# Loading the last full group in four chunks, counting landed chunks on ScalarE, and ten tail pieces instead of fourteen

## The reference

```python
keep = (u >= P_DROP).astype(x.dtype)          # P_DROP = 0.1
x_drop = x * keep / (1.0 - P_DROP)            # x, u: 8192 x 64, fp32
y = x + jnp.matmul(adj, x_drop)               # adj: 8192 x 8192, fp32
m = jnp.mean(y, axis=-1, keepdims=True)
v = jnp.var(y, axis=-1, keepdims=True)
out = (y - m) / jnp.sqrt(v + 1e-5)
```

## Time and profile before

| | |
|---|---|
| median of 3 runs | 644.17 us (644.09 to 645.23) |
| the profiled execution's own time | 644.2 us |
| its span, from the first to the last instruction | 642.4 us |
| TensorE busy | 508.3 us, 79% |
| HBM read, written | 272.63 MB, 2.10 MB |
| mean granted TensorE clock | 0.906 |

### The profile page before, as it was taken

The page is one execution under the profiler, slowest core; times in us unless marked ns, Lnnn a source line. Parts: engine busy times, 40 slices in busy tenths (PEclk is TensorE's granted clock), DMA queues, the critical chain, the costliest instruction groups (busy, mean ns, idle before and its releaser), DMA issues.

```text
span 642.4 us, 7619 instructions
## 1 busy us (share of the span) xinstructions
PE 508.3 (79%) x3458; PEld 264.1 (41%) x3458; DVE 60.7 (9%) x268; ACT 19.6 (3%) x26; POOL 1.1 (0%) x8
## 2 busy tenths in 40 slices
PE   0088798798897698788788788787888788888997
PEld 0044344343444344444444443443444444434546
DVE  1200200200100200100100100100010200110112
ACT  0000000000000000000000000000000000000000
POOL 0000000000000000000000000000000000000000
PEclk9998988987989978978988988987979978978999
DMA  9999999999999999999999999999999999999997
GB/s 384 429 430 445 426 432 445 429 428 449 429 428 449 429 428 449 429 428 441 436 428 414 451 440 395 448 448 407 432 444 426 432 432 441 428 432 426 434 413 295
DMA packets 7780, 274.80 MB, mean 428 GB/s; under 512 B 992, under 2 KB 1504, under 8 KB 2272
## 3 DMA queue, kind: packets, MB, share of 16 engines
q1 hardware_dynamic: 7632, 274.70, 99.2%
q10 hardware_dynamic: 144, 0.03, 0.0%
HBM read 272.63 MB, written 2.10 MB: 428 GB/s over the span
## 4 chain that ended last, share of the span: by engine, by line
DMA 65%; PE 34%; DVE 0%; issue 0%; SPq 0%; ACT 0%
DMA adj_ring<-adj_blocks 65%; PE acc L203 29%; PE tail_acc L203 4%; PE back L210 0%; SPq L145 0%; DVE acc_sb L253 0%; PE final L235 0%; SPq L147 0%; DVE x_and_u L316 0%; PE final L246 0%; ACT std L193 0%; DVE stats L310 0%; PE final L241 0%; DVE mean_var L312 0%; DVE rstd L314 0%
## 5 line engine op out<-in xcount | busy, mean ns | idle before, releaser
L203 PE MATMUL acc<-adj_ring,x_and_u 128*64 128x320 f32 x3072 | 462.5, 466 | 118.8 <-DMA adj_ring<-adj_blocks 118.8
L203 PEld LDWEIGHTS acc<-adj_ring,x_and_u 128*64 128x64 f32 x3072 | 231.9, 148 | 344.2 <-DMA adj_ring<-adj_blocks 127.0
L253 DVE COPY acc_sb<-acc 128x320 f32<-128x320 f32 x24 | 10.7, 486 | 519.1 <-PE acc L203 519.1
L203 PE MATMUL tail_acc<-adj_ring,x_and_u 128*64 128x384 f32 (+1 forms) x250 | 27.8, 383 | 0.0
L210 PE MATMUL back<-twofold,acc_sb 128*128 128x64 f32 x126 | 16.8, 280 | 11.9 <-DVE acc_sb L253 11.9
L210 PEld LDWEIGHTS back<-twofold,acc_sb 128*128 128x128 f32 x126 | 15.0, 191 | 18.8 <-DVE acc_sb L253 18.6
L184 ACT ACTIVATE std<-squares,eps 128x5 f32<-128x5 f32 (+1 forms) x13 | 3.9, 300 | 613.6 <-DVE squares L278 613.6
L203 PEld LDWEIGHTS tail_acc<-adj_ring,x_and_u 128*64 128x64 f32 x250 | 15.9, 137 | 11.6 <-issue 11.4
L184 ACT ACT_TABLE_LOAD x12 | 15.4, 1283 | 1.2 <-POOL eps L171 1.0
L284 DVE TENSOR_SCALAR x_and_u<-summed,mean,rstd 128x64 f32 (+1 forms) x63 | 15.2, 308 | 0.5
L262 DVE BATCH_NORM_STATS2 stats<-summed 128x6 f32<-128x64 f32 x63 | 9.3, 213 | 0.4
(11 more groups left out here) (19 smaller groups left out, 5.8 us busy)
## 6 DMA issues: line engine op xcount, KB each, us to landing
adj_ring<-adj_blocks SPq DMA_DIRECT2D x24, 7680.0 KB, 33.4
adj_ring<-adj_blocks SPq DMA_DIRECT2D x12, 5120.0 KB, 36.9
adj_ring<-adj_blocks SPq DMA_DIRECT2D x1, 4992.0 KB, 26.6
x_and_u<-xu SPq DMA_DIRECT2D x1, 4096.0 KB, 12.2
adj_ring<-adj_blocks SPq DMA_DIRECT2D x1, 2880.0 KB, 15.9
adj_ring<-adj_blocks SPq DMA_DIRECT2D x1, 2112.0 KB, 20.6
out<-x_and_u SPq DMA_DIRECT2D x1, 1920.0 KB, 15.1
adj_ring<-adj_blocks SPq DMA_DIRECT2D x1, 1536.0 KB, 23.8
```

The costliest lines, as they stand in the source:

```text
L203: return nc.tensor.matmul(into[h * D:(h + 1) * D, 0:cols], x_drop[:, t * D:(t + 1) * D], adj_ring[:, at:at + cols], start=(t < 2), stop=(t ...
L253: last = nc.vector.tensor_copy(acc_sb[:, b * cols:(b + 1) * cols], part[:, 0:cols])
```

## The change

The last of the twelve groups is loaded in four chunks of 24, 20, 12 and 8 k tiles instead of three of 24, 24 and 16, each with a semaphore of its own. The eleven groups before it keep their three slots, and the slots are still released at 24, 48 and 64 k tiles.

TensorE's loop no longer waits for the DMAs. ScalarE waits for each chunk and adds to `tiles_ready` the number of stretches that it contains; TensorE waits for `tiles_ready` ahead of the k tiles 0, 24, 44, 48 and 56 of every group. ScalarE's `root` of group g - 1 stands behind its count for the first chunk of group g.

The tail's pieces become 24, 16, 10, 8, 6 and 20, 18, 14, 8, 4. The direct products are gone: all 64 k tiles of the last row tile are halved, and the folding product (now with `final_ready`) is the last one.

```diff
+LAST_TILES = [24, 20, 12, 8]
+WAITS = sorted(set(SLOT_FIRST + LAST_FIRST))
-TAIL = [(3, [26, 15, 11, 8, 4]), (1, [13, 16, 12, 8, 6, 4, 2, 2, 1])]
+TAIL = [(3, [24, 16, 10, 8, 6]), (1, [20, 18, 14, 8, 4])]
-DIRECT = 2
...
-            with sp.Fori(1, FULL) as group:
+            with sp.Fori(1, FULL - 1) as group:
                 for s in range(SLOTS):
 
                     sp.wait_ge(adj_used, (group - 1) * SLOTS + s + 1)
                     load(s, group)
+            for i, (before, count) in enumerate(zip(LAST_FIRST, LAST_TILES)):
+                at, width = before * TILE, count * TILE
+
+                slot = sum(at + width > first * TILE for first in SLOT_FIRST)
+                sp.wait_ge(adj_used, MAIN - 2 * SLOTS + slot)
+                sp.dma_start(adj_ring[:, at:at + width], block_of(FULL - 1, at, width)).then_inc(last_loaded[i], 16)
...
+            def tell(before, count):
+
+                stretches = sum(before <= first < before + count for first in WAITS)
+                act.sem_inc(tiles_ready, stretches)
+
             act.wait_ge(eps_ready, 1)
-            with act.Fori(0, FULL) as g:
-                root(g, R)
+            for s in range(SLOTS):
+                act.wait_ge(chunk_loaded[s], 16)
+                tell(SLOT_FIRST[s], SLOT_TILES[s])
+            with act.Fori(1, FULL - 1) as g:
+                for s in range(SLOTS):
+                    act.wait_ge(chunk_loaded[s], (g + 1) * 16)
+                    tell(SLOT_FIRST[s], SLOT_TILES[s])
+                    if s == 0:
+
+                        root(g - 1, R)
+            for i in range(len(LAST_TILES)):
+                act.wait_ge(last_loaded[i], 16)
+                tell(LAST_FIRST[i], LAST_TILES[i])
+                if i == 0:
+                    root(FULL - 2, R)
+            root(FULL - 1, R)
...
                 for s in range(SLOTS):
-                    pe.wait_ge(chunk_loaded[s], (g + 1) * 16)
                     for pair in range(SLOT_FIRST[s], SLOT_FIRST[s] + SLOT_TILES[s], 2):
+                        if pair in WAITS:
+                            pe.wait_ge(tiles_ready, g * len(WAITS) + WAITS.index(pair) + 1)
...
-                        if n < LAST or t < HALVED:
-                            last = product(tail_acc[n], rows * P, col, t, KT if n < LAST else HALVED)
-                        else:
-                            last = nc.tensor.matmul(final[:, 0:D], adj_ring[:, col:col + P],
-                                                    x_drop[:, t * D:(t + 1) * D], start=False, stop=(t == KT - 1))
+                        last = product(tail_acc[n], rows * P, col, t)
...
-                    if n == LAST and i == len(TAIL[n][1]) - 2:
-
-                        pe.wait_ge(acc_copied, FULL + LAST + 1)
-                        nc.tensor.matmul(final[:, 0:D], acc_sb[:, 0:P], twofold[:], start=False, stop=False)
+            pe.wait_ge(acc_copied, FULL + LAST + 1)
+            nc.tensor.matmul(final[:, 0:D], acc_sb[:, 0:P], twofold[:], start=False, stop=True).then_inc(final_ready, 1)
...
-            take([tail_acc[LAST]], P, MAIN + FIRST_PIECE[LAST] + len(TAIL[LAST][1]) - DIRECT)
-
-            dve.wait_ge(adj_used, MAIN + FIRST_PIECE[LAST] + len(TAIL[LAST][1]))
+            take([tail_acc[LAST]], P, MAIN + FIRST_PIECE[LAST] + len(TAIL[LAST][1]))
+            dve.wait_ge(final_ready, 1)
```

More of the change, by code:

```diff
@@ L21 @@
 SLOTS = len(SLOT_TILES)
+LAST_TILES = [24, 20, 12, 8]
+LAST_FIRST = [sum(LAST_TILES[:i]) for i in range(len(LAST_TILES))]
+WAITS = sorted(set(SLOT_FIRST + LAST_FIRST))
 MAIN = FULL * SLOTS
@@ L32 @@
 FIRST_PIECE = [sum(len(tiles) for _, tiles in TAIL[:n]) for n in range(len(TAIL))]
-DIRECT = 2
-HALVED = KT - sum(TAIL[LAST][1][-DIRECT:])
 X_PARTS = 4
@@ L40 @@
 assert FULL * R + sum(rows for rows, _ in TAIL) == KT
-assert all(sum(tiles) == KT for _, tiles in TAIL) and sum(SLOT_TILES) == KT
+assert all(sum(tiles) == KT for _, tiles in TAIL) and sum(SLOT_TILES) == sum(LAST_TILES) == KT
 def pieces(n):
@@ L62, in build @@
     out_rows = out.rearrange("(p t) d -> p (t d)", p=P)
-    adj_main = adj[0:FULL * P * RING].rearrange("(g c) -> g c", g=FULL)
+    adj_main = adj[0:(FULL - 1) * P * RING].rearrange("(g c) -> g c", g=FULL - 1)
     def slot_block(s):
@@ L67, in slot_block, with block_of @@
         return adj_main[:, first:first + width].rearrange("g (p c) -> g p c", p=P)
-    def tail_block(start, width):
-        first = (FULL * RING + start) * P
+    def block_of(group, start, width):
+        first = (group * RING + start) * P
         return adj[first:first + width * P].rearrange("(p c) -> p c", p=P)
@@ L113, in build @@
         chunk_loaded = [sem(f"chunk_loaded{s}") for s in range(SLOTS)]
+        last_loaded = [sem(f"last_loaded{i}") for i in range(len(LAST_TILES))]
+        tiles_ready = sem("tiles_ready")
         piece_loaded = [[sem(f"piece_loaded{n}_{i}") for i in range(len(tiles))]
@@ L134, in build @@
         normed_ready = sem("normed_ready")
+        final_ready = sem("final_ready")
         final_stats = sem("final_stats")
@@ L159, in _ @@
                     sp.wait_ge(adj_used, MAIN - SLOTS + slot)
-                    sp.dma_start(adj_ring[:, at:at + width], tail_block(at, width)).then_inc(piece_loaded[n][i], 16)
+                    sp.dma_start(adj_ring[:, at:at + width], block_of(FULL, at, width)).then_inc(piece_loaded[n][i], 16)
             sp.wait_ge(normed_ready, FULL)
@@ L200, in _, with product @@
         def _(pe):
-            def product(into, cols, at, t, end):
+            def product(into, cols, at, t):
                 h = t % 2
                 return nc.tensor.matmul(into[h * D:(h + 1) * D, 0:cols], x_drop[:, t * D:(t + 1) * D],
-                                        adj_ring[:, at:at + cols], start=(t < 2), stop=(t >= end - 2))
+                                        adj_ring[:, at:at + cols], start=(t < 2), stop=(t >= KT - 2))
             def turn_back(rows, done):
@@ L222, in _ @@
                             for t in (pair, pair + 1):
-                                last = product(acc[b], COLS, t * TILE + b * COLS, t, KT)
+                                last = product(acc[b], COLS, t * TILE + b * COLS, t)
                     last.then_inc(adj_used, 1)
@@ L335 @@
     for g in range(FULL):
-        for s, (before, count) in enumerate(zip(SLOT_FIRST, SLOT_TILES)):
+        tiles = SLOT_TILES if g < FULL - 1 else LAST_TILES
+        for i, count in enumerate(tiles):
+            before = sum(tiles[:i])
             put((g * RING + before * TILE) * P, g * R, R, before, count)
```

## The result

The changed kernel takes 643.23 us (median of 14 runs, 642.30 to 644.43) where the kernel before takes 644.20 (14 runs, 643.91 to 645.30): ratio 0.9981, 95% interval 0.9974 to 0.9988. The profiled execution took 643.32 us, with a span of 641.4.

The account below looks back on a forecast made before the run. DMA reading of adj bounds the kernel until 583.38, then TensorE. From 644.2 us, 2.6 at the tail's start, less 0.6 wait and 0.1 at the end, is 1.9; 1.8 by the statistics' starts was taken: 642.4, range 641.8 to 644.3.

Parts of the forecast that it names:

- What bounds the kernel: Whole loop: reading adj by DMA bounds it until 583.38, when the last group's second chunk has landed; then TensorE.
- the term 23.45 - 21.75: Last group's 40 k tiles behind the first chunk: full clock instead of half clock gains 1.7 us.
- Chunks, and the full clock behind them: Last group: second chunk lands at 580.32, the 2.70 us wait goes, 40 k tiles take 21.75 us, group ends 602.5.
- What is late next: Tail's first piece: lands at 606.4, TensorE starts at 606.45; of 4.3 us gained, 2.6 are left, 1.7 become a wait.
- ScalarE as counter: Relay of landings to TensorE: 0.1 us at the last group's first chunk, covered by the wait at 606.4.
- Fewer pieces, no direct products: Tail: four loads fewer taken as 0; halved products' end to statistics 0.94 us; dropping direct products costs 0.1.
- The sum: Whole kernel: 1.8 us, by the two starts of the statistics, off 644.2 gives 642.4; forecast's chance 0.50.
- rival 1: Tail's start: clock falls, 1.7 us more, 0.6 us wait absorbs its share, net 1.1, 643.5 us; chance 0.30.
- the clock at the tail's start: New gap of 0.95 us idle, 1.33 small products, 1.65 idle: full or half clock behind it left undecided.
- rival 2: Tail: clock stays down longer, 3.0 us less 0.6 against a gain of 1.8, giving 644.8 us; chance 0.06.
- Rival 3: Tail's last pieces: big store served beside them delays the last landing up to 4.5 us, 646.0 us; chance 0.05.
- Rival 4: Tail's start: TensorE isn't earlier, count late or queue uneven, so no gain, 644.2 us; chance 0.09.

Follow-up runs that it names:

- run 6: The kernel before with eight products of 320 columns, result unread, ahead of the wait for every group's second chunk: 642.52 us, ratio 0.9974.
- run 1: The changed kernel with ten products of 320 columns, result unread, between the last group's `turn_back` and the tail's first piece: 642.34 us, ratio 0.9975.
- run 7: Run 5's kernel with the last two pieces (4 and 2 k tiles) as direct products into `final`: 642.17 us, ratio 0.9970.
- run 5: The changed kernel with tail pieces of 16, 15, 12, 10, 7, 4 and 12, 16, 14, 10, 6, 4, 2: 642.25 us, ratio 0.9968.
- run 4: The changed kernel without ScalarE's counting; TensorE waits for the DMAs itself, last group written out: 643.16 us, ratio 0.9982.
- run 3: The kernel before with only the new tail: new lists of pieces, no direct products: 644.68 us, ratio 1.0003.
- run 9: The changed kernel with only 4 of the first 60 row tiles stored: 643.08 us, ratio 0.9983; its profiled execution took 642.31 us.
- run 2: The changed kernel with the old tail (pieces and direct products of the kernel before), keeping four chunks and ScalarE's counting: 644.11 us, ratio 0.9998.
- run 10: The changed kernel with the big store issued ahead of the last row tile's pieces, complete output: 648.85 us, ratio 1.0070.
- run 8: Run 5's kernel with only 4 of the first 60 row tiles stored, output incomplete: 641.85 us, ratio 0.9962.

## Why the prediction was right, and where it was not

**What bounds the kernel: right.** No chunk's start moved by more than 0.03 us before the last group's second. TensorE's start of the last group's second chunk, 2.70 us late and at half clock, was the place. Run 6 measures the clock's part alone, 644.2 to 642.5: 1.7 us, the term 23.45 - 21.75.

**Chunks, and the full clock behind them: right.** No wait at the second chunk, no half clock, group end 602.12 (forecast 602.5). In the profiled executions of runs 1 and 7 TensorE reached the second chunk earlier and waited 0.28 and 0.62 us for it; the 160 records behind took 21.75 us even so.

**What is late next: right.** The first piece lands at 606.40 (forecast 606.4), TensorE starts at 606.45. Run 5 confirms it from the other side: with 16 k tiles the wait disappears.

**ScalarE as counter, at 0.1 us and covered: right.** 0.10 measured; run 4 without it has the same time.

**Fewer pieces, no direct products: right.** From the end of the halved products to the statistics it is 638.11 - 637.17 = 0.94 us, as forecast. Run 3 shows no difference, but could not show 0.1.

**The sum: right for the case that it describes, but that case was not the likeliest.** The range held because it was drawn wide enough for rival 1. The step that failed is "the clock at the tail's start". I gave the full clock 0.50 and rival 1 0.30. The changed kernel's 14 runs are three at 642.30 to 642.58 (the forecast, 642.4), three at 642.75 to 643.06, six at 643.23 to 643.43 (rival 1: 643.5) and two at 644.28 and 644.43 (rival 2: 644.8). The median is rival 1's. That half clock is what parts them is shown by run 1, which fills the gap: 642.34, with all twelve runs within 0.6 us; and by two profiled executions of the same shape, 643.32 with half clock and run 9's 642.31 without. So the change moved the gap and its half clock from one place to another: 2.6 us of earlier start, of which in most executions the clock takes back 1.5 less the wait of 0.6 that it covers.

I had also put at 1.3 us what the measurement can tell from none, and faster at 0.53 by that limit. The measured 1.0 is under it, yet the interval excludes none.

What the rows of before would have allowed: a gap ahead of the tail of 0.95 us idle, 1.33 of small products and 1.7 to 2.0 idle. I counted the small products as something that may hold the clock. Ten of the twelve gaps ahead of a second chunk had half clock behind them. Run 2 has the same gap, 0.3 us longer in its last part (2.32 us), and none of its twelve runs is under 643.7, where one with full clock would be at 642.4. In that run the products in the middle did not make two harmless gaps of it.

The page cited, "TensorE: Matmul & The Clock Gate" of the Trainium skill (section "HAM oscillation — how this bites in real kernels"), had this as its rule: a wait for data between bursts, half rate after it, and a penalty of half the throttled time. The trace of the changed kernel agrees: 2.01 us of idle time, then a granted clock of 0.79, 0.50 and 0.86 in the three stretches from 606 to 612, so 1.7 us of clock missing where the products are 1.5 us late. Not every execution follows it: three of the 14 have the forecast's time. I gave half clock 0.36, rivals 1 and 2 together; by the rows of before and the 14 runs it deserved more than half.

**Rival 3, the store ahead of the last pieces: did not happen** (run 9: the time doesn't fall when the store is cut). It would have been dearer than I worked out, 4.6 us of loss instead of 1.8 (run 10): the store's 4.5 us were right, the clock behind the wait and TensorE's part of the end were left out. **Rival 4** did not happen either: the tail started 2.62 us earlier.

**What the kernel before was.** Beside runs 1 to 4 it was executed 35 times: 6 at 642.20 to 642.54, 17 at 643.88 to 644.35 and 12 at 644.97 to 645.36. The two upper groups lie 1.7 and 2.8 us above the first, which fits the lengths of the 160 records in the earlier trace rows (21.75, 23.4, and 24.5 as in run 3's profiled execution of 645.18). That the fastest six are those without half clock in the last group wasn't seen in a profile; run 6, with the half clock taken away, lies where they lie. So, as far as these runs tell, the kernel before is as fast as the changed kernel at its best when its clock happens to hold.

**What stays open.** Which executions keep the clock behind a gap of this kind. The five profiled ones part by the idle time at its end (1.43 and 1.50 us: full clock; 2.01, 2.32 and 2.36: half), and in those of the changed kernel, of run 4 and of run 9, where the tail's first piece lands within 0.1 us of the same time, it is TensorE that was ready at 604.44, 604.11 and 604.89. But five are few, no run set that time on purpose, and in the earlier trace rows the clock held behind a gap of 3.59 us. And whether run 5's order with a cheaper last store could reach 641.8 with the complete output; run 8 reaches it only by leaving stores out.

## What to carry to other kernels

A gap on TensorE just ahead of the part that it bounds can cost twice, once as the wait and once as half clock behind it; price both, and ask where the gap goes when it is moved, since the clock's part moves with it. Before a new order of the loads is tried, fill the gap: products whose result nobody reads kept the clock for the part that follows, at no cost where they ended before the landing (run 6) or a later wait absorbed the excess (run 1). Here that alone gave 1.7 us, and runs 1, 5, 6 and 7, which all keep the clock, lie within 0.35 us of each other. When the transfer ahead of a bounded stage is the wait, size its first piece so that it has landed when TensorE is ready (16 k tiles here, not 24), and look next at the stores, which cost 0.4 us here.

## What the runs showed of the hardware that was not expected

The five products of `turn_back` (ten records, 1.33 us) in the middle of a gap did not always hold the clock: between 608 and 610 the granted clock was 0.50, 0.63 and 0.50 in the profiled executions of the changed kernel, of run 2 and of run 4, and 1.00 in those of runs 9 and 10, whose gaps ended with 1.50 and 1.43 us of idle time where the others' ended with 2.01, 2.32 and 2.36.

SP's queue held up its issues with some ten loads outstanding: 0.34 to 0.43 us is the usual time to issue one, and one took 3.4 and one 9.6 in the kernel before, with the DMA engines busy all the time. A store that stood behind it was issued at 622.92, where the changed kernel with four loads fewer issued it at 608.31. It landed at the same time in both, 638.0 and 637.8, so this cost nothing here.
